# A transformer sandwich on one core: the residual's scaled attention rows through a PSUM bank, the masked row statistics on GpSimd, and a new written order

## The reference

```python
x = x + _layernorm(_L0_attn_ref(_layernorm(x), qkv_w, conv_w0, ..., ln_w, ln_b))
x = x + _layernorm(_L0_ffn_ref(_layernorm(x), w_gate, w_up, w_down, s_gate, s_up, s_down))
...
# attention: tokens of 16 channels, two branches of 8 channels, windows of 8 tokens
attn = softmax(q * scale @ k^T);  out = attn @ v + lepe(v)      # lepe: 3x3 depthwise
att = concat(x1, x2) @ proj_w + proj_b;  tok = tok + layernorm16(att) * ln_w + ln_b
# feed-forward on rows of 512
y = (silu(x @ w_gate * s_gate) * (x @ w_up * s_up)) @ w_down * s_down     # 512 -> 2048 -> 512
```

## Time and profile before

| | |
|---|---|
| median of 3 runs | 983.97 us (980.8 to 984.06) |
| the profiled execution's own time | 981.15 us |
| its span, first to last instruction | 979.4 us |
| mean granted TensorE clock | 0.975 |
| busy: PE, DVE, POOL, ACT | 908.9, 863.2, 761.2, 660.3 us |

### The profile page before, as it was taken

One profiled execution on the slowest core, in us unless ns is written; L12 is line 12 of the kernel. 1 busy time (PEld: TensorE's weight loads), 2 busy tenths in 40 slices (PEclk: granted clock), 3 DMA queues, 4 the chain that ended last, 5 costly groups with the idle time before them and its releaser, 6 DMA issues.

```text
span 979.4 us, 17776 instructions
## 1 busy us (share of the span) xinstructions
PE 908.9 (93%) x6527; PEld 705.8 (72%) x6527; DVE 863.2 (88%) x1088; ACT 660.3 (67%) x1151; POOL 761.2 (78%) x709
## 2 busy tenths in 40 slices
PE   4645799999999999999999999999999999999996
PEld 3534777878777777778777777777777777777774
DVE  5999999999999999999999999999999999993322
ACT  2778686767777676768677686867768585645332
POOL 3687688887889888888889888787987888777323
PEclk9867899999999999999999999999999999999998
DMA  5613130222203012221303212130302011111101
GB/s 120 195 43 77 31 84 4 66 65 53 78 23 108 23 44 65 66 65 33 98 23 71 57 46 65 44 88 1 93 16 63 25 44 44 45 43 44 45 1 44
DMA packets 68886, 54.94 MB, mean 56 GB/s; under 512 B 40384, under 2 KB 56768, under 8 KB 68800
## 3 DMA queue, kind: packets, MB, share of 16 engines
q1 hardware_dynamic: 63936, 53.49, 20.6%
q10 hardware_dynamic: 4864, 0.32, 0.3%
HBM read 37.02 MB, written 16.78 MB: 55 GB/s over the span
## 4 chain that ended last, share of the span: by engine, by line
PE 65%; DVE 13%; POOL 7%; issue 6%; ACT 5%; DMA 1%; ACTq 1%; POOLq 0%; DVEq 0%
PE ps_up L574 17%; PE ps_gate L574 16%; PE ps_acc L593 16%; PE ps_w L535 8%; DVE xr L1071 5%; DVE prod L993 3%; PE ps_w L555 3%; DVE fst L1076 2%; POOL sum L851 2%; PE ps_w L526 2%; PE ps_w L565 2%; PE ps_w L544 1%; DMA xr<-in_L_attn_x 1%; POOL frs L802 1%; ACT o L719 1%
## 5 line engine op out<-in xcount | busy, mean ns | idle before, releaser
L851 POOL TENSOR_TENSOR sum<-prod 128x1024 f32<-128x1024 f32 x128 | 302.2, 2365 | 41.8 <-DVE prod L993 31.3
L993 DVE TENSOR_TENSOR prod<-ps_x,qkvl 128x2048 f32<-128x2048 f32 x128 | 290.3, 2279 | 2.4 <-ACT ps_x L687 1.9
L593 PE MATMUL ps_acc<-wd,mid 128*128 128x512 f16 x1024 | 241.4, 379 | 0.0
L574 PE MATMUL ps_up<-xhi,wu 128*128 128x256 f16 x1024 | 230.6, 273 | 1.5 <-DVE mid L1094 1.5
L574 PE MATMUL ps_gate<-xhi,wg 128*128 128x256 f16 x1024 | 230.5, 273 | 0.0
L574 PE MATMUL ps_gate<-xlo,wg 128*128 128x256 f16 x1024 | 230.5, 273 | 0.0
L574 PE MATMUL ps_up<-xlo,wu 128*128 128x256 f16 x1024 | 230.5, 273 | 0.0
L755 ACT ACTIVATE mid<-ps_gate,sgate 128x256 f32<-128x256 f32 x256 | 106.7, 467 | 125.6 <-PE ps_gate L574 125.3
L919 POOL TENSOR_TENSOR mid<-mid 128x512 f16<-128x512 f32 x128 | 154.7, 1209 | 36.1 <-ACT mid L761 36.1
L593 PEld LDWEIGHTS ps_acc<-wd,mid 128*128 128x128 f16 x1024 | 100.2, 98 | 96.6
L1094 DVE SCALAR_TENSOR_TENSOR mid<-ps_up,sup,mid 128x256 f32<-128x256 f32 x256 | 110.6, 473 | 52.0 <-PE ps_up L574 43.7
(11 more groups left out here) (140 smaller groups left out, 1336.4 us busy)
## 6 DMA issues: line engine op xcount, KB each, us to landing
xrow<-in_L_attn_x SPq DMA_DIRECT2D x16, 512.0 KB, 3.7
xb<-in_L_attn_x SPq DMA_DIRECT2D x128, 64.0 KB
attn_rows<-ratt SPq DMA_DIRECT2D x32, 256.0 KB, 2.6
o<-attn_rows SPq DMA_DIRECT2D x32, 256.0 KB, 3.5
xr<-in_L_attn_x SPq DMA_DIRECT2D x16, 512.0 KB, 5.0
out_x<-y SPq DMA_DIRECT2D x15, 512.0 KB, 4.1
mid<-in_L_ffn_w_gate SPq DMA_DIRECT2D x1, 1024.0 KB, 5.6
mid<-in_L_ffn_w_up SPq DMA_DIRECT2D x1, 1024.0 KB, 8.1
```

Source lines behind the costliest of these rows:

```text
L574: mm = nc.tensor.matmul(ps[:, ROWS * i:ROWS * i + ROWS], w[:, k, P * j:P * j + P], xs[:, n % 2, k, :], start=(k == 0 and part == 0), stop= ...
L593: return nc.tensor.matmul(ps_acc[q][:], f[:, m % SPLITS, ROWS * i + P * q:ROWS * i + P * q + P], wd[:, 2 * m + i, :], start=(m == 0 and pa ...
L851: nc.gpsimd.tensor_tensor(sum4[:, u % 2, :].rearrange("p (s c) -> p s c", c=4), s[:, :, 0:4], s[:, :, 4:8], ALU.add).then_inc(half_done, 1)
L993: nc.vector.tensor_tensor(prod[:, half].rearrange("p (s j k) -> p s j k", j=WIN, k=WIN), left[:, :, None, :].broadcast_to([P, 4 * WIN, WIN ...
```

## The change

Three things are changed.

1. `norm1_add` becomes a step for each q, and a user of the work banks. ScalarE no longer scales `o1` in place: it writes the scaled rows, already in the layout of `xr`, to `ps_w0` (q = 0) or `ps_w1` (q = 1), after whoever used the bank last was read. VectorE adds that bank to `xr`. The next TensorE step on the bank waits for this addition (`xr_sum`).
2. The mask product of `spread` is on GpSimd instead of VectorE.
3. `START`, `PLAN` and `OWN` have new numbers, which move most steps a little.

```diff
-        WORK = ("spread", "xt", "qkv", "cat", "proj", "fx")
+        WORK = ("spread", "xt", "qkv", "cat", "proj", "norm1_add", "fx")
...
+            if name == "norm1_add":
+                return xr_sum, NQ * n + rest[0] + 1
...
-                (-10.50, ("ffn_norm1",)), (-6.36, ("norm1_add",)), (-5.51, ("ffn_norm2",)),
-                (-3.17, ("norm2_apply",)), (-2.10, ("fx", 0)), (-1.05, ("fx", 1)), (7.68, ("keep_x1",)),
...
+                (-17.87, ("cent_out",)), (-10.21, ("ffn_norm1",)), (-9.01, ("norm1_add", 0)),
+                (-6.78, ("norm1_add", 1)), (-6.76, ("ffn_norm2",)), (-3.38, ("norm2_apply",)), (-2.74, ("fx", 0)),
...
-            def norm1_add(n, bank):
+            def norm1_add(n, q, bank):
                 act.wait_ge(f_rs, 2 * n + 1)
-                for q in range(NQ):
-                    nc.scalar.activation(o1_rows(q), o1_rows(q), ACT.Copy,
-                                         scale=frs[:, 0, 0, q:q + 1]).then_inc(o1_scaled, 1)
+                if bank.last:
+                    need(act, *released(bank.last))
+                rows = o1_rows(q).rearrange("p ae (h w) -> p h ae w", w=WIN)
+                nc.scalar.activation(bank.ps[:].rearrange("p (h ae w) -> p h ae w", h=WIN // 2, w=WIN), rows, ACT.Copy,
+                                     scale=frs[:, 0, 0, q:q + 1]).then_inc(o1_scaled, 1)
...
+            def spread_stats(n, bank):
+                pool.wait_ge(row_rs, n + 1)
+                if n == 0:
+                    pool.wait_ge(rowsel_done, 1)
+                need(pool, ln1_done, n)
+                nc.gpsimd.tensor_tensor(rmask[:], hmask[:, None, :].broadcast_to([P, 4, WIN]),
+                                        rrs[:].rearrange("p b s -> p (b s)")[:, :, None].broadcast_to([P, 4, WIN]),
+                                        ALU.mult).then_inc(row_masked, 1)
...
-            def norm1_add(n, bank):
+            def norm1_add(n, q, bank):
                 dve.wait_ge(s_xr[n % 2], times(n))
-                for q in range(NQ):
-                    dve.wait_ge(o1_scaled, NQ * n + q + 1)
-                    sums = xr[:, n % 2, q, :].rearrange("p (h ae w) -> p h ae w", h=WIN // 2, w=WIN)
-                    rows = o1_rows(q).rearrange("p ae (h w) -> p h ae w", w=WIN)
-                    nc.vector.tensor_tensor(sums, rows, sums, ALU.add).then_inc(xr_sum, 1)
+                dve.wait_ge(o1_scaled, NQ * n + q + 1)
+                nc.vector.tensor_tensor(xr[:, n % 2, q, :], bank.ps[:], xr[:, n % 2, q, :], ALU.add).then_inc(xr_sum, 1)
```

More of the change, by code:

```diff
@@ L285, in sandwich_kernel @@
[L285 to L304, removed]
@@ new lines, in sandwich_kernel @@
+                 ("spread", 0), ("load_row", 1), ("load_row", 2), ("load_xb", 1), ("stats", 1), ("apply", 0),
+                 ("xt", 0, 0, 0), ("qkv", 0, 0, 0), ("qkv", 0, 0, 1), ("spread", 1), ("scale_sums", 0),
+                 ("load_row", 3), ("scale_pow2", 0), ("xt", 0, 0, 1), ("scale_row", 0), ("qkv", 0, 0, 2),
+                 ("qkv", 0, 0, 3), ("stats", 2), ("qx", 0, 0), ("xt", 0, 1, 0), ("xt", 0, 1, 1), ("apply", 1),
+                 ("scale_spread", 0), ("qkv", 0, 1, 0), ("qkv", 0, 1, 1), ("qkv", 0, 1, 2), ("load_weights", 0),
@@ new lines, in sandwich_kernel @@
+                 ("load_xb", 2), ("load_row", 4), ("qkv", 0, 1, 3), ("qx", 0, 1), ("xt", 1, 0, 0), ("qk", 0, 0),
+                 ("qk", 0, 1), ("xt", 1, 0, 1), ("spread", 2), ("stats", 3), ("cast", 0, 0), ("exp", 0, 0),
+                 ("scales", 0), ("qk_sum", 0, 0), ("qkv", 1, 0, 0), ("qk_sum", 0, 1), ("cast", 0, 1),
+                 ("qkv", 1, 0, 1), ("qk", 0, 2), ("softmax", 0, 0), ("cast", 0, 2), ("token_bias", 0),
+                 ("qkv", 1, 0, 2), ("qk", 0, 3), ("pv", 0, 0), ("qk_sum", 0, 2), ("cast", 0, 3), ("qk_sum", 0, 3),
@@ new lines, in sandwich_kernel @@
+                 ("load_xb", 3), ("cast", 0, 4), ("exp", 0, 1), ("pv", 0, 1), ("xt", 1, 1, 0), ("apply", 2),
+                 ("qkv", 1, 0, 3), ("qkv", 1, 1, 0), ("qx", 1, 0), ("xt", 1, 1, 1), ("cast", 0, 5), ("spread", 3),
+                 ("token_bias", 1), ("softmax", 0, 1), ("qkv", 1, 1, 1), ("cast", 0, 6), ("pv_sum", 0, 0),
+                 ("pv", 0, 2), ("qkv", 1, 1, 2), ("qkv", 1, 1, 3), ("load_row", 5), ("pv", 0, 3), ("pv_sum", 0, 1),
+                 ("pv_sum", 0, 2), ("att_store", 0), ("qk", 1, 0), ("qx", 1, 1), ("pv_sum", 0, 3), ("attn_out", 0),
@@ new lines, in sandwich_kernel @@
+                 ("recip", 0), ("xt", 2, 0, 0), ("xt", 2, 0, 1), ("qk", 1, 1), ("stats", 4), ("apply", 3),
+                 ("qk_sum", 1, 0), ("cat", 0, 0), ("qk", 1, 2), ("cat", 0, 1), ("qk", 1, 3), ("proj", 0, 0),
+                 ("proj", 0, 1), ("load_xr", 0), ("square", 0, 0), ("square", 0, 1), ("qkv", 2, 0, 0),
+                 ("qk_sum", 1, 1), ("cent_std", 0), ("exp", 1, 0), ("cast", 0, 7), ("cent_var", 0),
+                 ("qkv", 2, 0, 1), ("cast", 0, 8), ("softmax", 1, 0), ("xt", 2, 1, 0), ("cast", 0, 9),
@@ new lines, in sandwich_kernel @@
+                 ("load_xb", 4), ("qk_sum", 1, 2), ("cent_out", 0), ("qkv", 2, 0, 2), ("exp", 1, 1),
+                 ("cast", 0, 10), ("qkv", 2, 0, 3), ("qx", 2, 0), ("cast", 0, 11), ("pv", 1, 0), ("spread", 4),
+                 ("qk_sum", 1, 3), ("softmax", 1, 1), ("pv", 1, 1), ("xt", 2, 1, 1), ("token_bias", 2),
+                 ("pv", 1, 2), ("pv_sum", 1, 0), ("pv_sum", 1, 1), ("att_store", 1), ("qkv", 2, 1, 0),
+                 ("qkv", 2, 1, 1), ("ffn_norm1", 0), ("qkv", 2, 1, 2), ("pv", 1, 3), ("norm1_add", 0, 0),
@@ L943, in _ @@
                                     pattern=[[C, WIN + 2]], channel_multiplier=-1).then_inc(tokens_done, 1)
-            walk({"stats": stats, "scales": scales, "token_bias": token_bias, "qk": qk, "pv": pv, "attn_out": attn_out,
+            walk({"stats": stats, "spread": spread_stats, "scales": scales, "token_bias": token_bias, "qk": qk, "pv": pv, "attn_out": attn_out,
                   "cent_out": cent_out, "ffn_norm1": ffn_norm1, "ffn_norm2": ffn_norm2, "finish": finish,
```

147 lines of the change are left out of this document (72 added, 75 removed), and 16 rows, old and new, of the table OWN.

## The result

The changed kernel takes 978.49 us in the median (977.5 to 979.6, 4 runs), against 984.01 for the kernel before on the same chip (980.8 to 984.23, 4 runs): a ratio of 0.9952, with a 95% interval of 0.9929 to 0.9975. That is 0.5% faster, at the edge of what a measurement of this kernel can tell. The forecast was 970 us, with 963 to 978: a gain of 14, and less than half of it came.

The account below looks back on a forecast made before the run. TensorE's work bounds the long stage, with 14.9 us of gaps made by a lagging, nearly full VectorE. 981.15 - 9.7 (`fx` waits) - 2.6 (other waits) + 0 = 968.9, with half of 2.8 added 970 us; range 963 to 978.

Parts of the forecast that it names:

- I take no wait: At `spread`, behind GpSimd's mask product in the new order: no wait expected; bound 11 waits of 0.3 us, about 5 us.
- the other waits of the stage: Two `spread` waits, a late `fuse` and their refills, 5.2 us in all; half, 2.6 us, was taken as gain.
- the start: Lead-in to TensorE's first gate: net -1 to +2 us, taken as 0 with bounds of -3 and +3.
- The residual sum: VectorE's sum reading PSUM: 0.69 us each, the pair 1.4 instead of 3.5, 2.1 us less per tile.
- all eleven waits of `fx`: TensorE's `fx` waiting for ScalarE's normalised rows (L725), 0.88 us per period with refill: all go, 9.7 us gained.
- ScalarE's scaling: ScalarE writing the scaled rows to PSUM instead of SBUF: 0.71 us, nothing gained.
- The mask product: Moved to GpSimd: 0.25 us there, VectorE relieved of 0.7 per tile; only its place in GpSimd's order can cost.
- the walk of the new order by hand: New order worked through with the trace's durations: GpSimd has less ahead of the mask product and is 1.4 us early.
- The cruder sum: On the timeline of before, `fuse_lo`, two `finish_add` sums, then the mask product: done at 474.16, 0.3 us too late.
- The hold on the work banks: `xt` on `ps_w0` and `ps_w1` must follow VectorE's read; the walk leaves 2.9 and 3.7 us, price 0.
- The step from the profiled execution to the median: A median stood up to 2.8 us above the profiled execution; half of that was added to 968.9, giving 970 us.
- a new wait takes the old one's place: Rival 3, chance 0.16: `spread` behind `finish_add` (5 us), a start 3 us later, or both: 973 to 979 us.

## Why the prediction was wrong

The prices of the operations were right. The steps that failed are three terms of the sum that were taken too favourably: "I take no wait" at `spread`, a gain of half of 5.2 us for the other waits of the stage, and the start at 0.

- **The residual sum** was right: 0.69 us expected, 0.683 measured, and with it alone all eleven waits of `fx` went. The stage gained 13.0 us in the run with that part alone, for 12.3 forecast.
- **ScalarE's scaling** was right: 0.71 expected, 0.689 measured.
- **The mask product.** Its duration was right (0.25 for 0.242), and "GpSimd has over 8 us free in a period, so its busy time costs nothing; only its place can" was too. What failed is the walk of the new order by hand that made it 1.4 us early. It is 0.18 late. The walk went by the durations of before, in which the `cent` product has 1.22 us; in the new places it falls beside a halving and takes 3.04, 1.8 us more on VectorE. Whether that is all of the difference isn't shown: with the product at 1.91 us (`cent_out` moved) the mask product was ready 0.24 us before `spread`, not 1.4. The cruder sum, `finish_add` put on the timeline of before, had said 0.3 us late and a bound of 5 us: it was nearer. The cost is 0.45 us in a period, so 3.6 in the eight alike and 4.1 in all nine.
- **The other waits of the stage** were to give 2.6 us. The two long `spread` waits did go. From fx11 to fx15 the new places lose 4.0 us against before and 6.0 against the old places with the same sums: a 2.65 us wait for `fuse`, the half clock behind it, and waits of 0.3 to 0.6 us. The prediction said that these places were new, and did not walk them.
- **The start** was taken as 0 with bounds of -3 and +3; it is +2.7 in the profiled execution. The prediction had the direction of its terms, and not the clock of TensorE in the start, which alone moved the gate by 4 us between two executions. So how much of the 2.7 is the new `START` can't be said from one execution of each.
- **The hold on the work banks** was right at 0: no steady step waits for VectorE's read of the bank.
- **The sum.** With the mask product on VectorE the new order gains 12.5 us from the gate to fx11 (605.7 to 593.2), about what was forecast for the whole stage. The waits at `spread` take 4.1 of it, the stretch behind fx11 4.1, and the start 2.7. That leaves about the 1.5 of the two profiled spans.
- **The step from the profiled execution to the median** was put at +1.4 us, from the one case of before. In the kernel after it is -1.1 (979.6 and 978.49). So the medians differ by 5.5, and this part is luck of which execution was profiled.

The rival of "a new wait takes the old one's place" is the one that came, with `spread` behind `finish_add` and the later start as written there. What it lacked was the end, and its 973 to 979 holds the result only in its last microsecond. It was given 0.16, since the walk was trusted over the crude sum.

What stays open is how the mask product on GpSimd costs the old `START` its lead. In all four profiles with both, the first `spread` comes 1.0 to 1.4 us sooner than in the four with the mask product on VectorE (9.93 to 10.15 us, against 11.19 to 11.34), and TensorE then idles 5.6 to 6.2 us instead of 4.4 to 4.6. The twelve `qkv` matmuls behind it take 4.60 to 5.11 us instead of 2.91 to 2.98. That the earlier `spread` causes the slower matmuls is argued from these rows, and no run isolates it.

## What to carry to other kernels

A short operation moved to another engine costs what stands ahead of it in that engine's queue: 0.24 us of work cost 54 us (72 with the PSUM sums) in the old places, and still 4 in the new order. A wait of TensorE for a short operation is made of all the work ahead of it, here 1.9 us of `token_bias` and 2.5 of `finish_add`. If an operation is freed from a conflict between VectorE and GpSimd by a new order, walk every other VectorE operation with two SBUF inputs through the new order too, and give each the halving that it now stands beside. And when a change has separable parts, time each alone: one part here was worth 16 to 19 us, and the other two gave back 13.5 of them.

## What was not expected of the hardware

A wait of the same 2.65 us at the same place was followed by TensorE's half clock in four profiled executions (in the kernel after: an interval of 55.44 us, granted clock 0.97 over the 50 us around it) and not in two others (53.75 us, 1.00). The loss behind a wait of this size is so 0 or 1.3 us by chance. At 4.45 us the half clock followed in the period shown, and cost 1.8 us in the next twelve matmuls (1.61 and 2.76, against 0.87 and 1.73).

In the start the column of the granted clock can read 1.00 while matmuls go at half pace: eight `qkv` matmuls took 3.62 us in the kernel after at 25.30 and 1.99 at 24.25 in the kernel with `cent_out` moved, both with 1.00 in the windows around them. The column has nothing to go by there: the first clock record of the trace is at 30.75 us in the kernel after, and at 21.89 in the other. Behind it the pace is full in both (eight `qkv` at 31.04 in the kernel after take 1.99 us). Ahead of the first record the duration of a known group tells the clock, not the column.
